# First attention of a vision transformer: the router's four tiles in four column groups, one mask product an image

## The reference

```python
h = patches @ w.T + b                        # 14 x 14 patches of 16 x 16 pixels: 196 tokens of 128 an image
q = _bitlinear(_layernorm(h), Wq); k = ...; v = ...        # quantised linear maps
scores = jnp.einsum('bqd,bkd->bqk', q, k) * B ** (-0.5)
scores = jnp.where(causal, scores, -jnp.inf)
h = h + jnp.einsum('bqk,bkd->bqd', softmax(scores), v)
logits = _layernorm(h).reshape(-1, 128) @ Wr               # 8 experts; layer 0's feed forward takes its top k from them
```

## Time and profile before

| | us |
|---|---|
| median of 3 runs | 2002.51 (2000.64 to 2004.06) |
| profiled execution | 2003.38 |
| its span | 2001.7 |
| TensorE busy | 1703.6 (85%) |
| VectorE busy | 1224.1 (61%) |
| GpSimd busy | 1138.6 (57%) |
| ScalarE busy | 1071.5 (54%) |

### The profile page before, as it was taken

One profiled execution on the slowest core, in us unless ns is written; L12 is line 12 of the kernel. 1 busy time (PEld: TensorE's weight loads), 2 busy tenths in 40 slices (PEclk: granted clock), 3 DMA queues, 4 the chain that ended last, 5 costly groups with the idle time before them and its releaser, 6 DMA issues. The chain is left out here.

```text
span 2001.7 us, 44426 instructions
## 1 busy us (share of the span) xinstructions
PE 1703.6 (85%) x13083; PEld 1263.3 (63%) x13084; DVE 1224.1 (61%) x4791; ACT 1071.5 (54%) x2510; POOL 1138.6 (57%) x1037
## 2 busy tenths in 40 slices
PE   4999999984448874599999999999982899998996
PEld 2566655653426653266766767667662798998985
DVE  2889988873741000589999999999965222322221
ACT  2666666652415442366666676666741455555553
POOL 2444444432245885125666666666656487877776
PEclk8999999996559887699999999999996899999998
DMA  8988899931013342201111121111112576776774
GB/s 202 208 218 210 213 212 215 217 87 57 0 36 52 66 64 35 78 26 48 46 50 52 47 54 47 50 54 44 44 39 68 116 137 125 137 134 121 136 133 79
DMA packets 270771, 198.08 MB, mean 99 GB/s; under 512 B 25326, under 2 KB 251152, under 8 KB 270608
## 3 DMA queue, kind: packets, MB, share of 16 engines
q1 hardware_dynamic: 220624, 160.65, 32.0%
q0 software_dynamic: 49984, 35.38, 13.0%
HBM read 143.33 MB, written 52.40 MB: 98 GB/s over the span
## 5 line engine op out<-in xcount | busy, mean ns | idle before, releaser
L2271 POOL DMA_INDIRECT out_dram<-r_yw,r_idx x212 | 328.4, 1549 | 121.4 <-issue 61.0
L2143 POOL DMA_INDIRECT rows_scratch<-routed_row,slot_u x256 | 252.5, 986 | 205.9 <-DVE slot_u L2094 142.0
L1817 ACT ACTIVATE a_probsT<-a_p_sc 98x392 f32<-98x392 f32 x384 | 173.5, 503 | 151.2 <-PE a_p_sc L1598 96.0
L2339 ACT ACTIVATE r_hT<-r_p_up,r_b1T 128x256 f32<-128x256 f32 x424 | 191.5, 473 | 113.4 <-PE r_p_up L2313 81.2
L2300 PEld LDWEIGHTS r_p_y<-w_all,r_hT 128*128 128x128 f32 x1696 | 223.1, 192 | 11.1
L2300 PE MATMUL r_p_y<-w_all,r_hT 128*128 x1696 | 223.6, 275 | 0.0
L2313 PE MATMUL r_p_up<-r_xgT,r_w1e 128*128 128x256 f32 x848 | 221.5, 385 | 0.6 <-ACT r_xgT L2344 0.6
L415 PE MATMUL p_embed<-pix,w_pix 96*128 96x392 f32 x512 | 208.1, 513 | 3.5 <-ACT pix L530 3.5
L680 POOL TENSOR_SCALAR vare<-mv 98x4 f32<-98x4 f32 x64 | 30.4, 476 | 229.5 <-DVE mv L665 195.4
L1914 DVE TENSOR_REDUCE a_negmax<-a_p_max 98x2 bf16<-98x392 f32 x256 | 132.1, 556 | 44.9 <-PE a_p_max L1565 40.6
L2356 DVE TENSOR_TENSOR r_yb<-r_p_y,b_all 128x256 f32<-128x256 f32 x106 | 45.0, 425 | 186.1 <-PE r_p_y L2300 156.3
(11 more groups left out here) (367 smaller groups left out, 4125.8 us busy)
## 6 DMA issues: line engine op xcount, KB each, us to landing
img<-in_x_dram SPq DMA_DIRECT2D x192, 196.0 KB, 4.2
img<-in_x_dram SPq DMA_DIRECT2D x192, 189.0 KB, 4.4
r_w1e<-in_L_ffn_W_dram SPq DMA_DIRECT2D x106, 256.0 KB
r_xg<-rows_scratch SPq DMA_DIRECT2D x106, 130.0 KB
xn_scratch<-xn SPq DMA_DIRECT2D x32, 196.0 KB
h_scratch<-h SPq DMA_DIRECT2D x32, 196.0 KB
h<-h_scratch SPq DMA_DIRECT2D x32, 196.0 KB
h3b<-h_scratch SPq DMA_DIRECT2D x32, 196.0 KB
```

The costliest lines, as they stand in the source:

```text
L1817: act.activation(probsT[:, u % 2, i, :], p_sc[i % 2][:, 0:2 * PAIR], ACT.Exp).then_inc(exped, 1)
L2143: pool.indirect_dma_start(rows_dram, bass.IndirectOffsetOnAxis(ap=slot_u[:, u % ROWS, c, t:t + 1], axis=0), row[:, u % ROWS, c, t, :], Non ...
L2271: pool.indirect_dma_start(acc_dram, bass.IndirectOffsetOnAxis(ap=idx[:, (k - 3) % 4, t:t + 1], axis=0), yw[:, (k - 3) % 4, t, :], None, co ...
L2339: act.activation(hT[:, (k - 1) % 2, f, :], p_up[f][:, 0:G], ACT.Silu, bias=b1T[:, bass.ds(e * FC + f, 1)]).then_inc(act_h, 1)
```

## The change

The router of a unit is no longer one product of 392 columns into 8 rows. Its four tiles are four products of 98 columns, and tile t goes to rows 32t to 32t+7 of `p_mm`, columns 0 to 97. So `lg` has 104 rows and 98 columns for each of its two buffers; ScalarE copies 104 x 98 in one instruction, rows between the groups included. SyncE stores a unit's logits with four DMAs of 8 x 98 instead of one of 8 x 392, and the counts of `lg_stored` are four times as high. The layout in DRAM stays.

In the scores of an image the two score products come first, and the second is made without a start flag. Then one product of the identity with `mask_qk`, read twice, writes both masked blocks: columns 0 to 97 and 196 to 293 of the bank.

```diff
@@ -245,7 +245,8 @@
         rstd2 = S("rstd2", [TILE, 2, TPU])
         xn2 = S("xn2", [TILE, 2, TPU, D])
         xn2T = S("xn2T", [D, 2, COLS])
-        lg = S("lg", [EXPERTS, 2, COLS])
+        LG_ROWS = 32 * (TPU - 1) + EXPERTS
+        lg = S("lg", [LG_ROWS, 2, TILE])
 
         p_embed = P("p_embed", [128, 512])
         p_htr = P("p_htr", [TILE, TPU, D])
@@ -395,10 +396,14 @@
                     u = n - 6
                     r = (k - 6) % 2
                     wait(sp, lg_ready, u + 1)
-                    sp.dma_start(logits_dram[:, span(u * COLS, COLS)], lg[:, r, :]).then_inc(lg_stored[r], 16)
+                    for t in range(TPU):
+                        sp.dma_start(logits_dram[:, span(u * COLS + t * TILE, TILE)],
+                                     lg[32 * t:32 * t + EXPERTS, r, :]).then_inc(lg_stored[r], 16)
             straight(sp, emit, DEPTH + 2, UNITS)
-            for s in (*xn2_stored, *h2_stored, *lg_stored):
+            for s in (*xn2_stored, *h2_stored):
                 sp.wait_ge(s, 16 * UNITS // 2)
+            for s in lg_stored:
+                sp.wait_ge(s, 16 * TPU * UNITS // 2)
 
         def emit_pe(pe):
             def patch(n, k, js):
@@ -468,12 +473,14 @@
                         q0, q1 = (slice((2 * m + i) * TILE, (2 * m + i + 1) * TILE) for i in range(2))
                         keys = slice(2 * m * TILE, (2 * m + 2) * TILE)
                         U, V = uT[:, (k - 2) % 2, :], xdT[:, (k - 2) % 2, :]
-                        pe.matmul(p_score[m][:, 0:TILE], U[:, q0], V[:, q0], start=True, stop=False)
-                        pe.matmul(p_score[m][:, 0:TILE], ident_b[0:TILE, 0:TILE], mask_qk[:],
-                                  start=False, stop=True)
-                        pe.matmul(p_score[m][:, TILE:CAUSAL], U[:, q1], V[:, keys], start=True, stop=False)
-                        last = pe.matmul(p_score[m][:, 2 * TILE:CAUSAL], ident_b[0:TILE, 0:TILE], mask_qk[:],
-                                         start=False, stop=True)
+                        pe.matmul(p_score[m][:, 0:TILE], U[:, q0], V[:, q0], start=True, stop=False,
+                                  skip_group_check=True)
+                        pe.matmul(p_score[m][:, TILE:CAUSAL], U[:, q1], V[:, keys], start=False, stop=False,
+                                  skip_group_check=True)
+                        diagonal = p_score[m][:, 0:4 * TILE].rearrange("p (b c) -> p b c", b=2)[:, :, 0:TILE]
+                        last = pe.matmul(diagonal, ident_b[0:TILE, 0:TILE],
+                                         mask_qk[:].unsqueeze(1).to_broadcast([TILE, 2, TILE]),
+                                         start=False, stop=True, skip_group_check=True)
                     last.then_inc(scored, 1)
                 patch(n, k, [4])
                 if live(n, 3, UNITS):
@@ -509,8 +516,10 @@
                     wait(pe, xn2T_ready, u + 1)
                     if live(n, 3, UNITS):
                         wait(pe, mixT_ready, u + 2)
-                    pe.matmul(p_mm[0:EXPERTS, 0:COLS], wr_sb[:], xn2T[:, (k - 4) % 2, :],
-                              start=True, stop=True).then_inc(routed, 1)
+                    for t in range(TPU):
+                        last = pe.matmul(p_mm[32 * t:32 * t + EXPERTS, 0:TILE], wr_sb[:],
+                                         xn2T[:, (k - 4) % 2, t * TILE:(t + 1) * TILE], start=True, stop=True)
+                    last.then_inc(routed, 1)
             straight(pe, emit, DEPTH, UNITS)
 
         def by_column(k, js):
@@ -583,8 +592,8 @@
                     u = n - 4
                     wait(act, routed, u + 1)
                     if not isinstance(u, int) or u >= 2:
-                        wait(act, lg_stored[k % 2], (u // 2) * 16 if isinstance(u, int) else (u - (k % 2)) * 8)
-                    act.copy(lg[:, k % 2, :], p_mm[0:EXPERTS, 0:COLS]).then_inc(lg_ready, 1)
+                        wait(act, lg_stored[k % 2], (u // 2) * 16 * TPU)
+                    act.copy(lg[:, k % 2, :], p_mm[0:LG_ROWS, 0:TILE]).then_inc(lg_ready, 1)
             straight(act, emit, DEPTH + 1, UNITS)
 
         def bcast(a, w):
```

## The result

The changed kernel is slower. Over eight runs each, its median is 2021.8 us and that of the kernel before 2004.1; the ratio is 1.0097, 95% interval 1.0078 to 1.0116, so 16 to 23 us. The forecast was 2016.5 (2008 to 2024), with 0.82 on slower.

A forecast was written before the change was run, and what follows sets the result against it. A two-unit loop through stores and image loads, not one engine, sets the pace: +1.3 and -0.2 us make 0.55 a period, 25 x 0.55 = 13.8, less 0.8 slack, plus 1 at the end: +14 on 2002.5, 2016.5 us (2008 to 2024).

The forecast's parts named there:

- The ring: Loop over two units, xn store, logits store, image loads, pixel copy, next xn; claimed to set the pace, 12.9 us a period.
- A: From the xn store through logits store and twelve image loads to the dependent pixel copy; about 13.7 us, predicted to grow 1.3.
- B: From the pixel copy to the xn store that depends on it; 12.17 us, predicted to shrink by 0.2.
- Part 1: SyncE's queue: three more logits stores a unit ahead of the image loads, 0.43 us each, add 1.3 us to A.
- Rival 2: SyncE's three added issues cost the ring next to nothing; 2001 us, no change; chance 0.10.
- Part 2: ScalarE's copy of lg, 98 columns for 392, lets hcur start sooner; B shrinks by 0.2 us (bounds 0 and 0.25).
- Part 3: TensorE's router product in four groups stays covered by the wait for hT, 0.09 us to spare; no time gained.
- rival 1: TensorE's router product outgrows its cover through exposed weight loads, B grows by 0.37 us; 2023 us; chance 0.10.
- Part 4: TensorE's scores: one mask product an image for two saves at most 0.1 us a unit, counted as 0.
- Rival 4: The two-block mask product runs at a quarter of the pace, B + 0.2 us; 2021.5 us; chance 0.05.
- The floor: Store to store distance the engines keep without a late image, 12.57 us; slack of periods there estimated at 0.8 in all.
- Rival 5: TensorE's clock falls in the stage, as in its last slices without patches; over 2030 us; chance 0.02.

## Why the prediction was right, point by point

**The ring.** That two successive distances add up to A + B is no finding: A and B are measured so that they must. What could have failed is that B keeps its value while the pixels come later, and that A takes the added issues. Both held: with four stores alone the median of B stayed at 12.17 and A went from 13.84 to 15.44. It was the step that made the forecast: the sign came from seeing that the added issues stand before the loads, behind a wait. One name in it is off: behind the stores of pass n stand the loads of unit n+1, not n+2; the distances measured are the right ones.

**Part 1, three issues, 1.3 us.** Right: four stores in 1.64 us for 0.39. The first image load came 2.76 us behind the `xn` store for 1.39 (means of all passes), 1.37 later; the twelve issues behind it then took 7.24 for 7.39, so that A rose from 13.84 to 15.05, 1.21. The stores alone gave the time of the whole change. The page counts 1536 more packets of the hardware queue, 48 a unit where the prediction had 24; that they cost nothing that the time shows is seen in the run with the logits ahead of the wait. Rival 2 fell: the image transfer started later by each issue. The Trainium skill ("DMA: Bandwidth & Descriptors", section on issuing engines not being separate DMA queues) calls the time to initiate a DMA usually small beside the DMA; here three of them, 1.37 us, made the kernel 1% slower where they stood ahead of the loads, and with the logits ahead of the wait the same issues cost nothing that the time shows (0.9971).

**Part 2, the short copy, 0.2 us.** Right: 0.24 us for 98 columns (estimated 0.25 to 0.28), B from 12.17 to 11.97.

**Part 3, the router.** Right that it is covered, and rival 1 fell. The passes did run side by side: 0.35 us for eight. The trace agrees with the Trainium skill ("TensorE: Matmul & The Clock Gate", section on packing small matmuls) that groups of columns overlap, and neither the forecast nor the result turned on it. The products and the short copy were never run apart from each other; that the products gain nothing in the ring is read from the turn, which starts 0.64 us after the start of `hT` for 0.65 before.

**Part 4, the mask.** Right in the ring, 0 (B 12.19, ratio 0.9986). The product with its output in two blocks took 0.25 us for 196 columns, where 98 took 0.21 in this row of the kernel before:

```profile
207.00 0.21 PE L472 MATMUL p_score<-mask_qk,ident_b 98*98 98x98 bf16 x1
```

From the first score of one image to that of the next it went from 0.64 to 0.60 us. Rival 4 fell, and the sentence of the Trainium skill ("PSUM — Partial Sum Buffer", specifications) that any non-contiguous access pattern slows matmuls significantly is not borne out by this one, with its two blocks of 98.

**The floor.** I had the floor of 12.57 us stay and take 0.8 us off the sum. It fell to 12.19 with the saved work of parts 2 to 4. In the kernels as given that is worth little, since only the passes with early pixels run at it.

**Rival 5, the clock, is the term that was mis-sized.** I gave it 0.02 as one large fall and left it out of the range. It came as a small one: in some passes in which the ring makes TensorE idle the clock falls, and B grows by 1.2 us and more. The profiled execution has it in three passes, at 309, 336 and 432 us. The sum of the stage was +14 and the profile gives +12.4 with these three in it; the median of the whole time gives +17.7. So the sum was a little too high for the profiled stage, although the clock was not in it. What put the median 5 us above the forecast is then sought in what the sum left out, the clock and the scatter behind the stage; how the two share it is not shown. The eight executions of the changed kernel lie between 2012.3 and 2037.3 us, those of before between 2000.2 and 2007.4, and, but for one pair of neighbours, the slower one of the changed kernel was, the lower its mean granted clock: 0.922 at 2012.3, 0.915 at 2021.0, 0.909 at 2030.5, 0.904 at 2037.3. That this is the clock in this stage in each of them is argued from the one that was profiled and from the runs with eight stores; the others were not profiled, and a long stretch at the lower clock behind the stage would show in the mean as well.

## What to carry to other kernels

A queue that only issues DMAs is an engine with an order like the others: what is put behind a wait and ahead of a load costs each issue nearly in full, 0.4 us here, though the queue idles 3 us a pass just before. Before an edit on a busy engine, find the loop that sets the pace (measure both ways between a load and the store that releases the next one), and see whether the edit shortens that loop or another. Here the edit was worth 0.37 us a pass, and showed it only when the loop through the loads had been opened by a change of order.

## What the runs showed of the hardware

Waiting can cost twice: a wait of TensorE of 1.8 us within a pass was followed by some 3 us at a granted clock of 0.50, which cost 1.2 us, and some 7 us at that clock cost 2 us and more. Eight useless products a pass, 1.9 us of work, made a kernel 1.1% faster. The length of a wait alone did not foretell it: the clock stayed at 1.00 through one of 2.36 us. Eight passes of 98 columns whose outputs go to four groups of rows of `p_mm` took 0.35 us with their eight weight loads, where six passes of 98 columns one behind the other took 0.67.
